# A non-local attention block on one core: images written out, products moved to block ends, a split first chunk, loads and units in another order

## The reference

```python
v = _gn(x)                                  # group norm, 32 groups of 8 channels
g_x = einsum('oc,bchw->bohw', g_w, v) + g_b          # 256 -> 128 channels
f = einsum('bnc,bcm->bnm', theta, phi)      # theta = phi = v: 4096 x 4096 per image
attn = softmax(f, axis=-1)
y = einsum('bnm,bmc->bnc', attn, g_x)
wy = einsum('oc,bchw->bohw', W_w, y) + W_b           # 128 -> 256 channels
wy = (wy - mean) * rsqrt(var + 1e-5) * gamma + beta  # mean, var over batch and positions
out = x + wy + v
```

## Time and profile before

| | us |
|---|---|
| timed runs: median of 3 (lowest, highest) | 2092.5 (2091.82, 2095.53) |
| the profiled execution, its own time | 2091.74 |
| span of the profile | 2090.0 |
| TensorE busy | 2027.0 |
| VectorE busy | 1543.7 |
| ScalarE busy | 1110.8 |
| GpSimd busy | 788.9 |

### The profile page before, as it was taken

How to read it: one execution, slowest core, us unless ns; L and a number is a source line. 1 busy time by engine, 2 the same in 40 slices (tenths; PEclk the granted TensorE clock), 3 DMA queues, 4 the chain that set the end, 5 groups by cost and what they waited for, 6 DMA issues and landing times.

```text
span 2090.0 us, 32328 instructions
## 1 busy us (share of the span) xinstructions
PE 2027.0 (97%) x9348; PEld 1453.2 (70%) x9348; DVE 1543.7 (74%) x3113; ACT 1110.8 (53%) x2312; POOL 788.9 (38%) x608
## 2 busy tenths in 40 slices
PE   5999999999999999999999999999999999999998
PEld 4787777666688777766678777766668877776443
DVE  5777777877777777787777677787777677777777
ACT  4345555566545445547553555546645544554656
POOL 4001233469601123458820122246970202344740
PEclk9999999999999999999999999999999999999999
DMA  3222334556411333565622223455551132346988
GB/s 126 112 90 87 106 117 126 177 165 207 163 68 72 121 101 104 160 201 158 215 82 82 82 94 129 131 177 161 186 187 66 66 121 94 99 131 200 338 297 346
DMA packets 107542, 300.29 MB, mean 144 GB/s; under 512 B 11488, under 2 KB 11872, under 8 KB 93536
## 3 DMA queue, kind: packets, MB, share of 16 engines
q1 hardware_dynamic: 107360, 298.11, 41.9%
HBM read 157.55 MB, written 140.51 MB: 143 GB/s over the span
## 4 chain that ended last, share of the span: by engine, by line
PE 75%; issue 8%; POOL 7%; DVE 4%; ACT 4%; DMA 1%; SPq 0%; ACTq 0%; DVEq 0%; POOLq 0%
PE bank L1357 13%; PE bank L1280 11%; PE bank L1282 11%; PE bank L1281 11%; PE bank L1333 8%; PE bank L1361 4%; PE bank L1363 4%; PE bank L1362 4%; PE bank L1516 3%; POOL fy_c L784 3%; POOL fy_d L784 3%; PE bank L1427 2%; ACT ring L863 2%; DVE plo L1098 1%; POOL xl L755 1%
## 5 line engine op out<-in xcount | busy, mean ns | idle before, releaser
L904 ACT CAST phi<-bank 128x512 fp32r<-128x512 f32 x480 | 281.3, 586 | 697.8 <-PE bank L1333 696.0
L1067 DVE TENSOR_SCALAR_CACHE_REDUCE ring<-bank 128x512 f32<-128x512 f32 x560 | 385.7, 690 | 269.0 <-PE bank L1282 197.5
L1280 PE MATMUL bank<-xh 128*128 128x512 f32 (+3 forms) x1152 | 513.8, 446 | 10.5 <-POOL xl L755 10.2
L1098 DVE TENSOR_TENSOR plo<-bank,phi 128x512 fp32r<-128x512 f32 x480 | 329.8, 687 | 153.4 <-ACT phi L904 107.3
L1282 PE MATMUL bank<-xh,xl 128*128 128x512 f32 (+3 forms) x1152 | 436.3, 379 | 0.0
L1281 PE MATMUL bank<-xl,xh 128*128 128x512 f32 (+3 forms) x1152 | 433.4, 376 | 0.0
L863 ACT ACTIVATE ring<-ring,nmax 128x512 f32<-128x512 f32 x464 | 334.2, 722 | 1.3
L784 POOL TENSOR_TENSOR fy_d<-fy_d,maxrow 128x512 f32<-128x512 f32 x181 | 234.6, 1299 | 254.8 <-DMA fy_d<-spill 254.8
L1333 PEld LDWEIGHTS bank<-ident,ring 128*128 128x128 f32 x1856 | 221.9, 140 | 150.4 <-issue 80.1
L784 POOL TENSOR_TENSOR fy_c<-fy_c,maxrow 128x512 f32<-128x512 f32 x192 | 248.1, 1295 | 175.3 <-DMA fy_c<-spill 175.1
L1333 PE MATMUL bank<-ident,ring 128*128 128x128 f32 x1856 | 281.3, 274 | 17.5 <-DVE plo L1098 15.1
(11 more groups left out here) (152 smaller groups left out, 2765.2 us busy)
## 6 DMA issues: line engine op xcount, KB each, us to landing
spill<-ring SPq DMA_DIRECT2D x108, 1024.0 KB, 4.3
fy_c<-spill SPq DMA_DIRECT2D x200, 256.0 KB, 4.0
fy_d<-spill SPq DMA_DIRECT2D x188, 256.0 KB, 4.1
ring<-x_dram SPq DMA_DIRECT2D x42, 512.0 KB, 4.9
lbuf<-spill SPq DMA_DIRECT2D x60, 256.0 KB, 3.7
yd<-yn SPq DMA_DIRECT2D x24, 256.0 KB, 3.4
out_dram<-ring SPq DMA_DIRECT2D x10, 512.0 KB, 3.0
fx_a<-x_dram SPq DMA_DIRECT2D x8, 512.0 KB, 6.5
```

Of the source, the lines that this page charges most:

```text
L904: nc.scalar.copy(phi[:, HI_BUF[n], :], whole(p)).then_inc(hi_made, 1)
L1067: last = nc.vector.tensor_scalar(slot_tile(u, t), src, 1.0, None, ALU.mult, ALU.max, accum_out=rowm[:, t, c:c + 1])
L1098: nc.vector.tensor_tensor(plo[:, n % LOS, :], whole(p), phi[:, HI_BUF[n], :].bitcast(F32), ALU.subtract).then_inc(lo_made, 1)
L1280: nc.tensor.matmul(dst, xh[:, k, rows], xh[:, k, cols], start=(k == 0), stop=False)
```

## The change

- The loop is gone on all five engines: every image is written out with constant targets. What the type test told is now told by `b == B - 1`, and on TensorE by the class `LastImage`.
- `PRODUCTS_FROM`: the products of block 2 begin 6 steps before the end of block 0 (before: at its end), those of block 3 in the last 4 steps of block 1, those of block 5 in the last 4 of block 3. The lengths change with them, so the last product of each block stays where it was. Four products of block 1 and one of block 3 lie a step earlier.
- `NEXT_AT`: the first product of the next image is in step 185, was 184; the other 31 follow up to the same last step.
- In the head, VectorE makes the second half of the first chunk (`xn`, `xh`, `xl`, each on 512 columns), ScalarE and GpSimd the first; TensorE waits for VectorE's half before its fourth matmul.
- The last loads: y of image 2, pieces 0 to 2, and x of image 3, pieces 0 and 2, are issued in steps 242 to 251 of the last image, behind `tile_used` of 241 to 250 (before: piece 2 of x in step 251, the others behind the last tile).
- `EMIT`: the units in the tail are scaled, added and stored in the order 4, 5, 6, 7, 0, 8, 9, 10, 1, 11, 12, 13, 2, ...; TensorE's order of units stays.

```diff
@@ -72,7 +72,7 @@
 
 BEFORE = {u: max((v for v in range(u) if SLOT[v] == SLOT[u]), default=None) for u in range(len(CHUNKS))}
 
-PRODUCTS_FROM = {j: (j - 1) * TPB for j in range(1, NB)} | {6: 5 * TPB - 8, 7: 5 * TPB + 8}
+PRODUCTS_FROM = {j: (j - 1) * TPB for j in range(1, NB)} | {2: TPB - 6, 3: 2 * TPB - 4, 5: 4 * TPB - 4, 6: 5 * TPB - 8, 7: 5 * TPB + 8}
 
 PRODUCTS = [(j, c, t) for j, c in CHUNKS for t in range(T)]
 PRODUCT_NO = {jct: s for s, jct in enumerate(PRODUCTS)}
...
@@ -171,7 +171,7 @@
     at = {}
     for j in range(1, NB):
         n = T * (NB - j)
-        steps = range(PRODUCTS_FROM[j], PRODUCTS_FROM[j] + {1: 22, 2: 19, 3: 18, 4: 18, 5: 18, 6: 2 * n, 7: 2 * n}[j])
+        steps = range(PRODUCTS_FROM[j], PRODUCTS_FROM[j] + {1: 20, 2: 25, 3: 22, 4: 18, 5: 22, 6: 2 * n, 7: 2 * n}[j])
         where = [s for s in steps if not tile(s)[3]]
         more = [s for s in steps if tile(s)[3]]
...
 STATS_OF = {s: c for c, s in enumerate(STATS_STEP)}
-NEXT_AT, NEXT_TO = XN_STEP[0] + 5, TILES - 18
+NEXT_AT, NEXT_TO = XN_STEP[0] + 6, TILES - 18
 NEXT_PRODUCTS = {NEXT_AT + q * (NEXT_TO - NEXT_AT) // (T * NB - 1): x for q, x in enumerate(PRODUCTS[:T * NB])}
 assert XN_STEP[0] > max(PRODUCT_STEP.values()) + 1 and len(NEXT_PRODUCTS) == T * NB and len(STATS_OF) == NB
...
@@ -353,10 +353,15 @@
 
 FIN_AT |= plan_final()
 G_HALF = (NB - 1) * TPB + ORDER[NB - 1].index((NB // 2 - 1, T - 1))
-ROW_8 = SLOT_USE[NB] + 1
-LATE_X = {1: max(TILES - 8, ROW_8 + 1), 2: max(TILES - 5, G_HALF + 2)}
-FIN_AT |= {s: (True, 3, q) for q, s in LATE_X.items() if s < TILES}
-assert len(FIN_AT) == 5 * FQ + sum(s < TILES for s in LATE_X.values())
+ROW_USED = {row: max(LEFT[w] for w in range(NLEFT) if LEFT_BUF[w] is not None and LEFT_BUF[w] >= LBUFS
+                     and SPARE_ROWS[LEFT_BUF[w] - LBUFS] == row) for row in SPARE_ROWS}
+LATE_FREE = {(False, 2, q): max(ROW_USED[0, 2 * q], ROW_USED[0, 2 * q + 1]) + 1 for q in range(FQ - 1)} | \
+    {(True, 3, 0): max(ROW_USED[1, c] for c in range(2 * K)) + 1, (True, 3, 2): G_HALF + 1}
+LATE_AT = {}
+for _piece in sorted(LATE_FREE, key=lambda piece: LATE_FREE[piece]):
+    LATE_AT[max(max(LATE_AT, default=0), LATE_FREE[_piece]) + 1] = _piece
+assert len(FIN_AT) == 5 * FQ and not set(FIN_AT) & set(LATE_AT) and max(LATE_AT) < TILES
+FIN_AT |= LATE_AT
 assert min(s for s, piece in FIN_AT.items() if piece[:2] == (False, 0)) > max(SLOT_USE[0], SLOT_USE[1]) + 1
 assert min(s for s, piece in FIN_AT.items() if piece[:2] == (False, 1)) > max(SLOT_USE[2], SLOT_USE[3]) + 1
...
+
+def plan_emission():
+
+
+    rest = list(range(KEPT, len(UNITS)))
+    order, rest = rest[:4], rest[4:]
+    for u in range(KEPT):
+        order += [u] + rest[:3]
+        rest = rest[3:]
+    return order + rest
+
+
+EMIT = plan_emission()
+assert sorted(EMIT) == list(range(len(UNITS)))
...
             n = b * NLEFT + w
-            return n - sum(v < w for v in VSUBS) if isinstance(b, int) and b == B - 1 else n
+            return n - sum(v < w for v in VSUBS) if b == B - 1 else n
 
         def kept(u, h):
...
                 step(0, s, True)
-            with sp.Fori(0, B - 1) as b:
+            for b in range(B - 1):
                 for s in range(HEAD, TILES):
...
             sp.wait_ge(left_added, B * NLEFT)
-            for q in range(FQ):
-                load_final(False, 2, q)
-            for q in range(FQ):
-                if LATE_X.get(q, TILES) >= TILES:
-                    load_final(True, 3, q)
-            for u, (b, q, k, h, n) in enumerate(UNITS):
+            for piece in [(False, 2, q) for q in range(FQ)] + [(True, 3, q) for q in range(FQ)]:
+                if piece not in LATE_FREE:
+                    load_final(*piece)
+            for n_out, u in enumerate(EMIT):
+                b, q, k, h, n = UNITS[u]
                 cols = slice(q * FW + h * W, q * FW + (h + n) * W)
-                sp.wait_ge(fin_added, u + 1)
+                sp.wait_ge(fin_added, n_out + 1)
                 sp.dma_start(outd[b, :, k, cols].rearrange("p (a w) -> p a w", w=W), unit_x(u)).then_inc(fin_out, 16)
             sp.wait_ge(fin_out, 16 * len(UNITS))
...
                 cols = slice(c * W, (c + 1) * W)
                 pool.wait_ge(xh_made, n * NB + c + 1)
-                nc.gpsimd.tensor_tensor(xl[:, :, cols], xraw(c), xh[:, :, cols].bitcast(F32),
+                mine = slice(0, 1) if (n, c) == (0, 0) else slice(0, K)
+                nc.gpsimd.tensor_tensor(xl[:, mine, cols], xraw(c)[:, mine, :], xh[:, mine, cols].bitcast(F32),
                                         ALU.subtract).then_inc(xl_made, 1)
...
-                for k in range(K):
+                for k in range(1 if (n, c) == (0, 0) else K):
                     last = nc.scalar.activation(xraw(c)[:, k, :], xraw(c)[:, k, :], ACT.Identity,
...
-                nc.scalar.copy(xh[:, :, cols], xraw(c)).then_inc(xh_made, 1)
+                mine = slice(0, 1) if first and c == 0 else slice(0, K)
+                nc.scalar.copy(xh[:, mine, cols], xraw(c)[:, mine, :]).then_inc(xh_made, 1)
 
...
             nc.vector.tensor_tensor(wgl[:, :, :], wraw, wgh[:, :, :].bitcast(F32), ALU.subtract).then_inc(wg_lo, 1)
+            dve.wait_ge(gn_bias, K)
+            nc.vector.tensor_scalar(xraw(0)[:, 1, :], xraw(0)[:, 1, :], gst[:, 3, 1:2], gst[:, 4, 1:2], ALU.mult, ALU.add
+                                    ).then_inc(head_xn, 1)
+            dve.wait_ge(head_xn, 1)
+            nc.vector.tensor_copy(xh[:, 1, 0:W], xraw(0)[:, 1, :]).then_inc(head_xh, 1)
+            dve.wait_ge(head_xh, 1)
+            nc.vector.tensor_tensor(xl[:, 1, 0:W], xraw(0)[:, 1, :], xh[:, 1, 0:W].bitcast(F32), ALU.subtract
+                                    ).then_inc(head_xl, 1)
             group(0, 3)
             dve.wait_ge(wg_lo, 1)
...
-            for u, (b, q, k, h, n) in enumerate(UNITS):
-                if (k, h) == (0, 0):
-                    if b == B - 1:
-                        act.wait_ge(fin_x_last[q], 16 * K)
-                    elif q == 0:
-                        act.wait_ge(fin_x[b], 16 * K * FQ)
+            for n_out, u in enumerate(EMIT):
+                b, q, k, h, n = UNITS[u]
+                if b == B - 1:
+                    act.wait_ge(fin_x_last[q], 16 * K)
+                elif b not in [UNITS[v][0] for v in EMIT[:n_out]]:
+                    act.wait_ge(fin_x[b], 16 * K * FQ)
                 nc.scalar.activation(unit_x(u), unit_x(u), ACT.Identity, scale=gnp[:, b, 1, k:k + 1],
                                      bias=shift[:, b, k:k + 1]).then_inc(fin_scaled, 1)
...
+                    if first and s == 0 and k == 1:
+                        pe.wait_ge(head_xl, 1)
                     nc.tensor.matmul(dst, xh[:, k, rows], xh[:, k, cols], start=(k == 0), stop=False)
                     nc.tensor.matmul(dst, xh[:, k, rows], xl[:, k, cols], start=False, stop=False)
...
                         else:
-                            pe.wait_ge(fin_added, u - 3)
+                            pe.wait_ge(fin_added, EMIT.index(u - 4) + 1)
                         if (q, k, first) == (0, 0, 0) and b < B - 1:
                             pe.wait_ge(fin_y[b], 16 * FQ)
                     at = q * FW + (first + h) * W
```

34 lines of the change are left out of this document (20 added, 14 removed).

## The result

Four runs of the changed kernel had a median of 2063.42 us (2062.11 to 2065.24) against 2092.16 (2090.3 to 2095.53) of the kernel before, ratio 0.9861, 95% interval 0.9844 to 0.9879. The forecast was 2071.5, its range ended at 2064.5: right in direction, 8 us too small in size. Over all runs of this study the changed kernel lies at 2064.5 (12 runs, 2062.1 to 2065.8) and the one before at 2091.9 (40 runs, 2088.7 to 2095.7), 27.5 us apart. The profiled execution took 2062.11 around a span of 2060.4, 29.6 less than before.

A forecast was written before the change was run, and what follows sets the result against it. TensorE was taken as the bound, busy 97% of the span, with 63 us idle to close. Terms 2.1 + 4.8 + 1.5 + 5.4 + 1.6 + 2.6 + 2.2 = 20.2 off 2091.74 gave 2071.5 us; range 2064.5 to 2079.

The forecast's parts named there:

- block 1's end: Wait of 0.49 us before step 60's transpose; the new products begin behind that transpose, so nothing gained.
- the clock's 1.5 us: Behind image 2's jump back, 3.4 us at granted clock 0.50; half is 1.7, of which 1.5 was counted as gain.
- `xl` wait: TensorE's 1.49 us before the next image's first product; one tile put ahead gains 2.6 over three images, leaving 0.3 to 0.8.
- 38 to 42, 68 to 72: Steps of blocks 1 and 2 left without products: cost 0; rival had waits move there, 2078.5 us, chance 0.16.
- slower to feed: Rival: written-out code pays a late fetch at each instruction buffer refill, above all on TensorE; 2113 us, chance 0.03.
- Jumps: Loop jumps back after step 12 in images 1 and 2 go, low clock included; gain 4.8 us.
- tail: Last units: serving bank units first on VectorE removes TensorE's idle of 2.06 before its matmuls; gain 2.2 us.
- the head: First chunk split between ScalarE with GpSimd and VectorE; first product at about 22.8, gain 2.1 us (1.6 to 2.3).
- the meeting of the two subtractions: In the first chunk, VectorE's and GpSimd's subtractions contend for SBUF; on GpSimd it would cost up to 0.7 us.
- part 3: Moved products cover TensorE's waits: 5.4 us at block 0's end, 1.6 at block 3's, over four images.
- Registers: Computing semaphore targets in the looped images goes away; gain 1.5 us for three images, with 0 and 5 as ends.
- registers cost more: Rival: slower VectorE and ScalarE handoffs, another 1.5 us per image in blocks 4 to 7; 2065 us, chance 0.14.

The follow-up runs named there:

- The loops alone: Kernel before the change with all images written out and nothing else changed; 2084.25 us, ratio 0.9963.
- the late loads alone: Kernel before the change with only the last loads moved into block 7 of the last image; 2093.23 us, ratio 1.0002.
- the products alone: Kernel before the change, loop kept, with only the products of blocks 1, 2, 3 and 5 moved; 2081.77 us, ratio 0.9951.

## Why the prediction was right or wrong

**Right by place.** Every wait that the forecast said would go went, none took its place, and the one at block 1's end stayed as it said. TensorE's idle came to 43.5 where it said near 45; the sum took all but the clock's 1.5 us out of the idle, while the busy time fell by 10.1. Of the `xl` wait 0.3 to 0.8 was to stay; it went whole at the product, and 0.28 stands before the tile ahead of it. The places forecast at nothing for a new wait (38 to 42, 68 to 72) stayed without one, and the longer program was not slower to feed: the larger instruction queue moved 76 packets and 1.25 MB, fewer than before. Jumps, `xl` and tail came within 0.2 us of their terms, the head within its error. The loss of up to 0.7 at the meeting of the two subtractions did not come: VectorE was first there, the case that the prediction priced at 1.6, and the first product came 2.1 earlier.

**Wrong in size, on one side.** Of the 8.1 us between the forecast and the first four runs, 1.0 is that those four lie below the 12; the terms have the rest.
- *Block ends and step 19, 11.9 for 7.0.* The step that failed is the counting of part 3. It prices a moved product only as cover for a wait of TensorE, and the new lengths not at all. The shorter spread of block 1 takes a product's work off VectorE at step 19: 1.7 for nothing. "That gains nothing" at block 1's end was right on the wait and 1.0 off on the time. At block 0's end "1.38 is lost" per image was measured between one pair of rows; step by step the stretch gives 1.66, 6.5 in all for 5.4, since the transposes behind it had been late too. Block 3's end gives 2.7 for 1.6; 0.2 of that is the loop's.
- *Registers, 3.2 for 1.5.* The comparison of images 1 and 3 gave 0.7 an image for half of it, I counted 0.4 of that and little for the second half. The loops alone have 1.3 an image, 0.2 of it at block 3's end. The rival "registers cost more", 2065, came nearest by its number, but its mechanism is only half of it: it had the `xl` wait go whole and 1.5 us in blocks 4 to 7 of each image; there the loops alone gave 0.3 an image, and nothing at the `xl` wait.
- *Blocks 6 and 7, 2.4 for 0, in the profiled execution.* Most of this is chance, not the change: the same changed kernel gives 70.9 to 73.8. The mean of the 13 profiles is 73.0; the profile before was at 73.3 and the first after at 70.9. Without it the profiles differ by 27.2, and the medians of all runs by 27.5.

So with the terms as measured the forecast would have been 2091.74 - 27.2 = 2064.5, the median of the 12 runs. That is the very end of the range, so the 1.0 by which the first four runs lie below is luck, and the 7 us above it are not. The range of 2064.5 to 2079 was too high because I took each block end at its two rows and each unlooked-at place at zero; errors of that kind have one sign.

## What to carry to other kernels

When work is moved from one step to another, read all steps of the block in the trace of before, for the short waits that recur in every image too, and follow both ends of every stretch that is moved or resized, on the engine that waits and on the engines that answer it: 0.17 us of wait, four times over, was worth 1.7, and it went because VectorE had less to do there. Before a difference in a stretch is put down to a change, take a second profile of the same kernel; here up to 4 us of 73 came and went without any edit, 1.2 of them with two instructions 0.02 us apart. And where a stretch is bound by an engine that hands rows over one by one, count what the two engines that share the rows do to each other before giving one of them more.

## What the runs showed of the hardware

- A wait of TensorE is sometimes paid twice, once as idle time and once at the lower clock. The jump of image 2 in the kernel with the late loads alone has the same wait as before the change (1.64 and 1.60), and no low clock behind it (granted 1.00 from 1117.8 to 1121.2, where it was 0.50 before); that kernel's tail has the same wait as before (2.05 and 2.06), where no low clock followed, and here one did, as in the tail of the products alone. Its timeline, and the window (columns as above):

```profile
1117.71 0.65 PE L1336 MATMUL bank<-ident,ring 128*128 128x128 f32 x4 [1.64 <-issue]
...
2044.55 4.11 PE L1519 MATMUL bank<-ring,wwt 128*128 128x512 f32 x5 [2.05 <-DVE fx_a L1255]
```

```profile
2044.55:2049.55 5.00, 5.00 (x8) 2.22 (x9) 4.80 (x4) 5.00 (x6) 0.00 (x0) 0.66 1.01 406
```

  Five matmuls took 4.11 us where each is 0.43 at full clock, and the tail was 1.7 longer. The kernel before had a mean clock under 1.000 in 20 of the 36 executions that ran beside the experiments, the changed kernel in none of 12. Part of what the waits cost is so a matter of chance in each execution, and gone with the waits.
- A subtraction on VectorE with both operands in SBUF takes 0.68 us alone; started during GpSimd's, it ends 0.52 to 0.62 after it in 198 of 211 cases, whatever the rest of that one is (0.68 to 1.79 in all), and in 6 after the next one (1.86).
- The loop's code, with semaphore targets computed in registers, costs 1.3 us an image over straight code, in seven places of 0.09 to 0.25 us. The two jumps back cost 4.9 more, low clock included.
